# A 32-row tail product for four batches at once, in place of the seventh product of each tile

## The reference, cut to what matters

```python
para = conv1x1(x, pw) + pb;  para = relu(para)
para = conv3x3(para, cw) + cb                       # 16 bases for each pixel
xu = patches(x, 3, 3)                               # 32 channels x 9 taps
t = einsum('goje,bgjp->bgoep', Wb, xu)              # for each pixel 32 outputs x 16 bases
out = einsum('bgoep,bep->bgop', t, para)            # weighted sum over the bases
```

## Time and profile before

| | us |
|---|---|
| median of 3 runs | 391.56 (389.49 to 391.85) |
| the profiled execution | 389.57 |
| its span, first to last instruction | 387.7 |
| PE busy | 362.8 (94%) |
| DVE busy | 258.6 (67%) |
| ACT busy / POOL busy | 63.6 / 98.4 |
| mean granted clock of PE | 0.987 of full speed |

### The profile page before, as it was taken

The page is one execution under the profiler, slowest core; times in us unless marked ns, Lnnn a source line. Parts: engine busy times, 40 slices in busy tenths (PEclk is TensorE's granted clock), DMA queues, the critical chain, the costliest instruction groups (busy, mean ns, idle before and its releaser), DMA issues.

```text
span 387.7 us, 8951 instructions
## 1 busy us (share of the span) xinstructions
PE 362.8 (94%) x3434; PEld 257.3 (66%) x3434; DVE 258.6 (67%) x452; ACT 63.6 (16%) x148; POOL 98.4 (25%) x248
## 2 busy tenths in 40 slices
PE   4899999999999999999999999799999979799991
PEld 3558888888888888888888888423266742467670
DVE  4776777977878878878788788634334276912255
ACT  1125010010100100101001000420032059452200
POOL 4537777888600000000000000115001029400000
PEclk9999999999999999999999999989999999999996
DMA  7654757527347176174382000288700000000032
GB/s 228 169 141 118 202 130 196 153 55 200 100 122 203 29 181 167 32 198 124 87 212 52 0 0 0 57 196 218 169 0 3 3 0 2 0 3 5 3 111 109
DMA packets 28640, 38.58 MB, mean 99 GB/s; under 512 B 7072, under 2 KB 23776, under 8 KB 27936
## 3 DMA queue, kind: packets, MB, share of 16 engines
q1 hardware_dynamic: 18080, 27.52, 27.8%
q10 hardware_dynamic: 10528, 10.61, 10.4%
HBM read 4.56 MB, written 2.10 MB: 17 GB/s over the span
## 4 chain that ended last, share of the span: by engine, by line
PE 78%; DVE 7%; SPq 5%; DMA 3%; issue 2%; ACT 2%; ACTq 2%; POOL 1%; DVEq 0%; POOLq 0%
PE ps L882 23%; PE ps L883 23%; PE ps L886 8%; SPq L360 5%; PE ps L1072 5%; PE ps L1056 5%; PE ps L933 3%; PE ps L1001 3%; PE ps L1025 2%; DMA X<-in_x 2%; PE ps L857 2%; PE ps L917 2%; PE ps L1041 1%; ACTq L383 1%; PE ps L991 1%
## 5 line engine op out<-in xcount | busy, mean ns | idle before, releaser
L882 PE MATMUL ps<-WA,HS 128*128 128x512 f32 x384 | 153.6, 400 | 0.0
L883 PE MATMUL ps<-WB,LS 128*128 128x512 f32 x384 | 150.7, 392 | 0.0
L1161 DVE TENSOR_TENSOR PROD<-ps,PT 128x512 f32<-128x512 f32 x128 | 88.4, 691 | 38.6 <-PE ps L886 32.7
L1145 DVE TENSOR_REDUCE RED<-PROD 128x32 f32<-128x512 f32 x128 | 86.4, 676 | 0.0
L882 PEld LDWEIGHTS ps<-WA,HS 128*128 128x128 f32 x384 | 72.4, 189 | 18.3
L883 PEld LDWEIGHTS ps<-WB,LS 128*128 128x128 f32 x384 | 72.4, 189 | 14.9
L886 PE MATMUL ps<-WC,TS 96*128 96x512 f32 x128 | 50.6, 395 | 0.0
L491 POOL MEMSET IMG<- 128x67 f32 x1 | 0.2, 153 | 138.7 <-DVE X L1151 138.7
L733 ACT ACTIVATE HS<-HS 32x40 fp32r<-32x40 f32 x21 | 5.7, 274 | 163.3 <-DMA TS<-LO 163.0
L933 PE MATMUL ps<-SK,WE 128*32 128x512 f32 x256 | 28.7, 603 | 0.6 <-DMA SK<-IMG 0.6
L886 PEld LDWEIGHTS ps<-WC,TS 96*128 96x128 f32 x128 | 24.0, 188 | 5.2
(11 more groups left out here) (225 smaller groups left out, 332.3 us busy)
## 6 DMA issues: line engine op xcount, KB each, us to landing
LS<-HS SPq DMA_DIRECT2D x7, 960.0 KB, 5.7
HS<-HI SPq DMA_DIRECT2D x60, 80.0 KB, 2.4
SK<-IMG SPq DMA_DIRECT2D x32, 131.8 KB, 2.7
HS<-LO ACTq DMA_DIRECT2D x32, 80.0 KB, 2.6
LS<-LO ACTq DMA_DIRECT2D x32, 80.0 KB, 2.7
HS<-HI SPq DMA_DIRECT2D x30, 79.8 KB, 2.5
TS<-LO SPq DMA_DIRECT2D x34, 63.8 KB, 3.9
out_x<-OT SPq DMA_DIRECT2D x8, 256.0 KB, 2.1
```

The source lines that it names most:

```text
L882: pe.matmul(ps[b][:, :], px(HS, dy), WA[:, dy, :], start=(dy == 0), stop=False)
L883: pe.matmul(ps[b][:, :], px(LS, dy), WB[:, dy, :], start=False, stop=False)
L1145: ve.tensor_reduce(RED[j % 2][:, 32 * b:32 * b + 32], PROD[b % 2][:, :].rearrange("p (o e) -> p o e", e=E0), AX.X, ALU.add).then_inc(sum_d ...
L1161: ve.tensor_tensor(PROD[b % 2][:, :].rearrange("p (o e) -> p o e", e=E0), ps[b][:, :].rearrange("p (o e) -> p o e", e=E0), para.broadcast_ ...
```

## The change

The seventh product of every batch goes. In its place `low_products` opens each tile: for each dy and each batch one product of 32 rows, from a strip LR that holds LO shifted by two columns (no stacking over dy; partitions 32b to 32b+31 are batch b) and WC, which now holds the three dy of the third shift in each of the four row groups. Four of them, one for each batch, stand side by side in four row groups and write four banks; batch 3 alternates between ps3 and ps6 (`tile_bank`). LR is filled by one ScalarE copy for each strip (`low`; by DVE for the first one), and the 16 transfers of `stack_third` with their correction go: NREST 25 to 9. PE waits for the products of batches 0 to 2 of the last tile before the first 32-row products. DVE's order changes: reduce 3 of the last tile stands first, then the add of a chunk (`add_chunk`, tiles 1 and 5) or its statistics (`stats_chunk`, tiles 2 and 6), then product 0. At the start `stack_lo` of the first strip moves from ACT to SP, and WC's four row groups are filled by GpSimd (0, 1) and ScalarE (2, 3).

```diff
-NREST = 25
-FIRST_REST = NREST - 13
+NREST = 9
-        TS = [sb("TS0", [96, B, 2, SL // 2], F32R, at=img_at)[0], sb("TS1", [96, B, 2, SL // 2], F32R)[0]]
+        LR = [sb(f"LR{i}", [P, 2, S0], F32R)[0] for i in range(2)]
-        WC = sb("WC", [96, CH], F32R)[0]
+        WC = sb("WC", [P, 3, CH], F32R)[0]
+        def tile_bank(b, j):
+            return ps[6] if b == 3 and j % 2 else ps[b]
-        def stack_third(queue, s, half, batches):
...
+        def low_rows(s):
+            return LO[:, :, bass.ds(s * (SL // 2) + 2, S0)].rearrange("p t (r c) -> p t r c", c=W)[:, :, :, 0:W - 1]
+        def low_strip(half):
+            return LR[half][:, :, :].rearrange("p t (r c) -> p t r c", c=W)[:, :, :, 0:W - 1]
 # SP
             sp.wait_ge(lo_done, 3)
-            stack_third(sp, 0, 0, (0, 1, 2))
+            stack_lo(sp, 0, 0, first_lo)
...
-                    stack_third(sp, 2 * it + half, half, (2, 3))
 # GpSimd
-            for dy in range(3):
-                gp.tensor_copy(WC[32 * dy:32 * dy + 32, :], WA[64:96, dy, :]).then_inc(w0_moved, 1)
-                gp.wait_ge(w0_moved, dy + 2)
+            for b in range(2):
+                gp.tensor_copy(WC[32 * b:32 * b + 32, :, :], WA[64:96, :, :]).then_inc(w0_moved, 1)
+                gp.wait_ge(w0_moved, b + 2)
 # ScalarE
-            act.wait_ge(lo_done, 3)
-            stack_lo(act, 0, 0, first_lo)
+            act.wait_ge(w0_split, 1)
+            for b in (2, 3):
+                act.activation(WC[32 * b:32 * b + 32, :, :], WA[64:96, :, :].bitcast(F32), ACT.Copy).then_inc(w0_by_scalar, 1)
+            def low(s, half):
+                act.activation(low_strip(half), low_rows(s).bitcast(F32), ACT.Copy).then_inc(strip_fixed[half], 1)
...
                     act.wait_ge(tile_done, (2 * it + half - 1) * B * STRIP_T)
+                    low(2 * it + half, half)
                     stack_lo(act, 2 * it + half, half, strip_rest[half])
-                    stack_third(act, 2 * it + half, half, (0, 1))
 # PE
+            def low_products(half, t, j, g, first):
+                r = t // 2 * 4 + t % 2
+                for dy in range(3):
+                    a = (r + dy) // 2 * W
+                    for b in range(B):
+                        p = slice(32 * b, 32 * b + 32)
+                        if dy == 0 and b < 3 and not (first and j == 0):
+                            pe.wait_ge(product_done, 4 * g + b - 3)
+                        if dy == 0 and b == 3 and not (first and j < 2):
+                            pe.wait_ge(product_done, 4 * g - 4)
+                        pe.matmul(tile_bank(b, j)[:, :], LR[half][p, (r + dy) % 2, a:a + P], WC[p, dy, :], start=(dy == 0), stop=False)
                 for dy in range(3):
-                    pe.matmul(ps[b][:, :], px(HS, dy), WA[:, dy, :], start=(dy == 0), stop=False)
-                    pe.matmul(ps[b][:, :], px(LS, dy), WB[:, dy, :], start=False, stop=False)
-                if third_late:
-                    pe.wait_ge(first_fixed, 4)
-                pe.matmul(ps[b][:, :], px(TS, 0), WC[:, :], start=False, stop=True).then_inc(tile_done, 1)
+                    pe.matmul(tile_bank(b, j)[:, :], px(HS, dy), WA[:, dy, :], start=False, stop=False)
+                    ins = pe.matmul(tile_bank(b, j)[:, :], px(LS, dy), WB[:, dy, :], start=False, stop=(dy == 2))
+                ins.then_inc(tile_done, 1)
+                    low_products(half, t, j, g, first)
                     for b in range(B):
-                        if not (first and j == 0):
-                            pe.wait_ge(product_done, 4 * g + b - 3)
-                        tile(half, t, b, first and j == 0 and b == 0)
+                        tile(half, t, b, j)
 # DVE
+                    if not (first and j == 0):
+                        reduce((j - 1) % 2, 3, 4 * g - 1)
+                    if not (first and j < STRIP_T):
+                        if j % STRIP_T == 1:
+                            add_chunk(2 * it - 1 + j // STRIP_T, 1 - j // STRIP_T)
+                        if j % STRIP_T == 2:
+                            stats_chunk(2 * it - 1 + j // STRIP_T)
                     for b in range(B):
                         product(j, b, it * STRIP_T + j // 2, 4 * g + b)
...
-                        elif not (first and j == 0):
-                            reduce((j - 1) % 2, 3, 4 * g - 1)
-                    if j == 1 and not first:
-                        finish_chunk(2 * it - 1, 1)
-                    elif j == 5:
-                        finish_chunk(2 * it, 0)
```

More of the change, by code:

```diff
@@ L211, in build @@
         w0_moved = sem("w0_moved")
+        w0_by_scalar = sem("w0_by_scalar")
         w1_mixed = sem("w1_mixed")
@@ L239, in build @@
         first_fixed = sem("first_fixed")
-        first_third = sem("first_third")
+        first_low = sem("first_low")
         first_lo = sem("first_lo")
@@ L443, in _ @@
             repeat_hi(1, 1)
-            sp.wait_ge(lo_done, 5)
-            stack_third(sp, 1, 1, (2, 3))
             sp.wait_ge(pt_done, 4)
@@ L505, in _ @@
                 step(gp.memset(HS[half][64:96, :, :, S0 - 1:S0].bitcast(F32), 0.0))
-                step(gp.memset(TS[half][:, :, :, SL // 2 - 1:SL // 2].bitcast(F32), 0.0))
+                step(gp.memset(LR[half][:, :, :].bitcast(F32).rearrange("p t (r c) -> p (t r) c", c=W)[:, :, W - 1:W], 0.0))
             gp.wait_ge(w_par, 16)
@@ L731, in fix @@
                 for m, p, c in ((HS, slice(0, 32), 0), (HS, slice(64, 96), W - 1), (HS, slice(96, 128), 0),
-                                (LS, slice(0, 32), 0), (LS, slice(64, 96), W - 1), (TS, slice(0, 96), W - 1)):
+                                (LS, slice(0, 32), 0), (LS, slice(64, 96), W - 1)):
                     act.activation(wrapped(m[half], p, c), wrapped(m[half], p, c).bitcast(F32), ACT.Copy, scale=0.0).then_inc(strip_fixed[half], 1)
             act.wait_ge(lo_done, 5)
+            low(1, 1)
             stack_lo(act, 1, 1, strip_rest[1])
-            stack_third(act, 1, 1, (0, 1))
             fix(1, 1, 16 * NREST)
@@ L742, in _ @@
                     act.wait_ge(tile_done, (2 * it + half - 1) * B * STRIP_T)
+                    low(2 * it + half, half)
                     stack_lo(act, 2 * it + half, half, strip_rest[half])
-                    stack_third(act, 2 * it + half, half, (0, 1))
-                    fix(half, it + 1, 16 * NREST * it + (16 * FIRST_REST if half == 0 else 16 * NREST))
+                    fix(half, it + 1, 16 * NREST * (it + half))
             def norm(out_ap, k0, k1, p=slice(0, P), c0=0, c1=W):
@@ L870, in _, with tile @@
                 ins.then_inc(pt_done, 1)
-            def tile(half, t, b, third_late=False):
+            def low_products(half, t, j, g, first):
[9 more added lines that the diff above has]
+                        pe.matmul(tile_bank(b, j)[:, :], LR[half][p, (r + dy) % 2, a:a + P], WC[p, dy, :], start=(dy == 0), stop=False)
+            def tile(half, t, b, j):
                 r = t // 2 * 4 + t % 2
@@ L902, in block0 @@
                         pe.wait_ge(first_repeat, 1)
+                        pe.wait_ge(first_low, 1)
                     elif t == 0:
                         pe.wait_ge(strip_fixed[half], NFIX * (it + half))
+                    low_products(half, t, j, g, first)
                     for b in range(B):
-                        if not (first and j == 0):
-                            pe.wait_ge(product_done, 4 * g + b - 3)
-                        tile(half, t, b, first and j == 0 and b == 0)
+                        tile(half, t, b, j)
                     if j > 0:
@@ L919, in _ @@
             pe.wait_ge(w0_split, 2)
-            pe.wait_ge(w0_moved, 4)
+            pe.wait_ge(w0_moved, 3)
+            pe.wait_ge(w0_by_scalar, 2)
             block0(0, True)
@@ L1119, in _ @@
             ve.wait_ge(lo_done, 3)
[L1120 to L1125, removed]
+            ve.tensor_copy(low_strip(0), low_rows(0)).then_inc(first_low, 1)
             ve.wait_ge(w0_split, 1)
@@ L1136, in _ @@
                     ve.memset(wrapped(HS[0], slice(96, 128), 0).bitcast(F32), 0.0).then_inc(first_fixed, 1)
-            ve.wait_ge(first_third, 4)
-            ve.wait_ge(strip_rest[0], 16 * FIRST_REST)
-            ve.memset(wrapped(TS[0], slice(0, 96), W - 1).bitcast(F32), 0.0).then_inc(first_fixed, 1)
             ve.wait_ge(pt_by_vector, 2)
@@ L1145, in reduce, with add_chunk @@
                 ve.tensor_reduce(RED[j % 2][:, 32 * b:32 * b + 32], PROD[b % 2][:, :].rearrange("p (o e) -> p o e", e=E0), AX.X, ALU.add).then_inc(sum_done, 1)
-            def finish_chunk(k, half):
+            def add_chunk(k, half):
                 ve.wait_ge(sums_transposed, STRIP_T * k + STRIP_T)
@@ L1151, in finish_chunk, with stats_chunk @@
                 ve.tensor_tensor(xs, sums_bank(half), xs, ALU.add).then_inc(x1_done, 1)
+            def stats_chunk(k):
                 ve.wait_ge(x1_done, k + 1)
-                ve.bn_stats(ST[:, bass.ds(k, 1), :], xs).then_inc(stats1_done, 1)
```

(6 more changed lines are left out.)

## The result

| | before | changed |
|---|---|---|
| median, us | 390.72 (389.49 to 391.85, 4 runs) | 396.48 (395.58 to 397.99, 4 runs) |
| the profiled execution, us | 389.57 | 397.99 |
| its span | 387.7 | 395.9 |

The ratio is 1.0137 with a 95% interval of 1.0088 to 1.0186: 3.4 to 7.3 us slower. The forecast was 395.0 and "slower". "us" is microseconds everywhere, "a slot" the distance from the start of one product to the start of the next.

The account below looks back on a forecast made before the run. PE was taken as the only bound in block 0; 1.04 us added less 0.925 removed per tile gave +3.7 us over 32 tiles, with +0.2 after the last tile +3.9. Forecast 395.0 us, range 385 to 402.

Parts of the forecast that it names:

- What bounds: Block 0's tiles: PE is the only bound, with DVE close behind; PE's cost per tile, times 32 tiles, can move.
- The tile: Block 0, PE: 1.04 us added and 0.925 removed, +0.115 a tile, so transposes 6.70 us apart instead of 6.58.
- Added: Start of each tile on PE: three rounds at 0.22 us (0.66) plus 0.40 for two height changes, less 0.02: 1.04 us.
- the 0.02 that I took off: In the added time per tile: the slot before the change in is cut to its bare stream, 0.02 us less.
- My second place: L1025 and L1041, alternating with two f32 rounds each: 0.36 us for a pair of changes, said to agree with 0.40.
- Removed: PE in each tile: four slots go, each 0.231 us (6.473 us for 28 products), 0.925 us in all.
- The signs: New profile: transposes 6.70 apart, two PEld idle spells a tile, first products 0.1 us longer, low products within 0.85 us.
- a rival for the kernel as it is: DVE late: batch 2's product ends 0.1 to 0.3 us after PE's change in, despite 0.45 cover; 398 to 404, chance 0.06.
- The outside of block 0: Queues, strip transfers and start: all hidden, zero effect with perhaps 0.5 us error; first tile still at 30.3.
- The sum: Whole kernel: +3.7 us over 32 tiles and +0.2 after the last tile, +3.9 us; forecast 395.0.
- Cheap changes: Rival: fp32r height changes cost little; with none of the 0.40, minus 9.1 us, about 382.7; chance 0.24, mostly partial size.
- Unclosed rounds: Rival: each round waits for its own loads, 0.105 us more for rounds two and three; 6.7 us, 401.7; chance 0.15.

Follow-up runs that it names:

- e5: The kernel before with only DVE's new order and the split of add and statistics; ratio 0.9982 to before, tile 6.591 us against 6.585.
- e2: The changed kernel with the twelve 32-row products issued twice in each tile; 417.66 us, tile 7.377 us, 0.697 more for three rounds.
- e1: The changed kernel with three full-height products (sums wrong) for the twelve 32-row ones; 382.94 us beside 392.2 for before, tile 6.286 us, 0.394 less than changed.
- e3: The changed kernel with batch 0's first full product put between rounds 2 and 3, same result; 409.25 us, tile 7.097 us, 0.416 more.
- e4: The changed kernel with DVE's order of before; 396.53 us, ratio 1.0109 to before, six tiles 0.34 to 0.45 us longer.

## Why the prediction was right, point by point

**What bounds.** Right: PE in block 0, and DVE's order alone changes nothing (e5).

**The tile.** 6.70 was forecast, 6.680 measured. The mechanism is the one forecast, but two terms were too small and cancelled; that the sum came so close is luck.

*Added*: 1.04 forecast, 1.11 measured. A round takes 0.232 (e2), not 0.22, and just past the upper bound of 0.231; that is 0.04 for three. I had halved the f32 stream and added too little of the surplus that a full product's slot has as well. The rest is the 0.02 that I took off and the pair itself, put at 0.40 from f32 rows: e1 and e3 bracket it with 0.394 and 0.416. So f32 and fp32r products pay about the same for it. My second place (0.36) was not the same shapes, as I had said, but 32*128 against 128*32, and it was too low.

*Removed*: four slots of 0.231 by the sum, 0.925 us. Measured it is 1.01. Before, 27 slots follow the first 0.34 us of a tile, 6.24 us in all; changed, 23 slots of 0.227 follow the first 1.45, 5.23 us in all. The removed products had also made their neighbours longer, so 0.09 more went with them. The step "a slot is a slot, 6.473 / 28" is the one that was mis-sized.

**The signs.** The twelve low products were to lie within 0.85 us from first start to last end; it is 0.98: 0.34 and 0.23 for the first two rounds, and 0.41 from the first start of the third to its last end, for a product lasts longer than a slot. The two idle spells of PEld and the 0.1 us at the first product on each side are there.

**DVE.** Product 2 was to end 0.45 before PE's change in. In the tile shown above it starts at 223.68 and ends at 224.37, and the load is at 224.79: 0.42. With the old order the cover is gone behind six of the seven chunks (e4). What I forecast as a rival for the kernel as it is happens only there.

**The outside of block 0.** Forecast: nothing, with an error of perhaps 0.5 us. The 16 transfers a strip that went (38.58 to 32.51 MB by the page of the profile) brought nothing, since strips were ready anyway. The start is some 0.5 us later on average, at the edge of that error. The landing in block 1 and the clock are the execution's. My condition that the time outside of block 0 should not differ by more than 1 us fails (4.9 us more in the profiled execution), and it was badly set: two executions of the same code differ by more than that.

**The sum.** 3.9 forecast, 3.4 to 7.3 measured. Block 0 alone has 3.3 in the traces (0.096 x 32 = 3.1, and 0.3 at the end, where I had put 0.2), just under the lower end of the interval; with the 0.5 at the start it is 3.8. The median's 5.8 is 2 above that. No part of the traces that belongs to the change accounts for these 2, and I put them down to scatter: e4, whose block 0 is 5.6 longer than before, is 4.3 slower by its ratio.

**The rivals.** Cheap changes: out by e1 and e3. It would have needed a pair under 0.285 by my sum, and under 0.32 by what was measured (1.01 less three rounds of 0.232). Unclosed rounds: out by e2 (0.232 against 0.33). The Trainium skill ("TensorE: Matmul & The Clock Gate", "Part 3: Packing small matmuls") has four row tiles at 3.07 times the speed of one after the other. The runs here differ: four take 0.232 where four full slots take 0.908, 3.9 times, as long as rounds follow each other. For the three rounds with the pair of changes it is 12 products in 1.11 us against 12 slots of 0.227: 2.45 times.

## What to carry to other kernels

Packing 32-row products side by side gives nearly four for one, but each stretch of them costs about 0.4 us for going in and out, some 1.8 slots of 512 columns here, so a stretch must save more slots than that: this one saved one (four for three). Price a change of height from a place in the trace where the same two shapes meet (f32 rows served for fp32r here), by the idle of PEld ahead of the first load and the first product's surplus. Where DVE frees banks that PE wants all at once, lay out both engines over one tile with the chunk work in it, for the cover may be gone in one tile of four only. And a product that is taken away may have cost more than its own slot: compare the slots beside it with slots far from it.

## What the runs showed of the hardware

- A pair of changes between full-height and 32-row products costs 0.39 to 0.42 us, of which some 0.11 on either side is the uncovered load and the rest the two gaps ahead of the loads.
- A product of 96 rows among products of 128 lengthens the slots around it, to 235, 233 and 232 ns or 232, 238 and 232 instead of 227. Filled up to 128 rows with zeros, the tile is 0.065 us shorter (0.046 where the product comes first) and the kernel 0.6% faster, with more data to multiply. What remains of the long slots, nearly half, is unexplained.
- In the kernel before, tiles vary between 6.55 and 6.66 us; in the changed one all are 6.678 to 6.689. In e1, which has no change of height either, they are 6.27 to 6.30, so it is not the changes that even them out.
